# A slot of every second block moved from TensorE's pick to Pool's gather, in the two aggregation phases of a graph network

## The reference, cut to what matters

```python
def mean_aggregate(x, src, dst, num_nodes):
    msgs = x[src]
    summed = jax.ops.segment_sum(msgs, dst, num_segments=num_nodes)
    deg = jax.ops.segment_sum(jnp.ones((src.shape[0],), x.dtype), dst, num_segments=num_nodes)
    return summed / jnp.maximum(deg, 1.0)[:, None]
```

## Time and profile before

| | us |
|---|---|
| median of 3 timed runs | 9398.32 (9396.81 to 9399.93) |
| the profiled execution's own time | 9389.86 |
| its span, first to last instruction | 9388.1 |
| PE busy in the span | 8537.5 (91%) |
| PEld busy | 7847.4 (84%) |
| POOL busy | 6558.1 (70%) |
| DVE busy | 6333.0 (67%) |
| ACT busy | 5621.9 (60%) |
| mean granted TensorE clock, share of full | 0.951 |

### The profile page before, as it was taken

One profiled execution on the slowest core, in us unless ns is written; L12 is line 12 of the kernel. 1 busy time (PEld: TensorE's weight loads), 2 busy tenths in 40 slices (PEclk: granted clock), 3 DMA queues, 4 the chain that ended last, 5 costly groups with the idle time before them and its releaser, 6 DMA issues. The chain is left out here.

```text
span 9388.1 us, 166017 instructions
## 1 busy us (share of the span) xinstructions
PE 8537.5 (91%) x52125; PEld 7847.4 (84%) x52126; DVE 6333.0 (67%) x7523; ACT 5621.9 (60%) x10160; POOL 6558.1 (70%) x6704
## 2 busy tenths in 40 slices
PE   6999999998879999999898878888888888999997
PEld 6999999888879999999888857777777777888886
DVE  4666666766766666667767666666666666777776
ACT  3666666555537666665555436666666666666664
POOL 3777777765637777777666447777777777777774
PEclk9999999999979999999999979899999999999998
DMA  3222222111112222221111122222222222222221
GB/s 61 48 49 48 49 47 50 42 39 36 39 29 50 47 48 49 47 50 44 40 38 37 31 70 57 57 56 54 57 57 57 57 57 57 55 55 57 57 57 50
DMA packets 404389, 466.17 MB, mean 50 GB/s; under 512 B 194789, under 2 KB 273209, under 8 KB 403942
## 3 DMA queue, kind: packets, MB, share of 16 engines
q0 software_dynamic: 212000, 156.07, 10.8%
q1 hardware_dynamic: 190388, 308.83, 10.5%
q10 hardware_dynamic: 1938, 0.49, 0.0%
HBM read 451.33 MB, written 13.55 MB: 50 GB/s over the span
## 5 line engine op out<-in xcount | busy, mean ns | idle before, releaser
L636 PE MATMUL banks<-split_sb,e_low_hot 128*128 128x400 f32 x20000 | 4283.2, 358 | 40.0 <-ACT e_low_hot L606 40.0
L636 PEld LDWEIGHTS banks<-split_sb,e_low_hot 128*128 128x128 f32 x20000 | 3796.7, 192 | 83.6 <-ACT e_low_hot L606 40.5
L855 POOL DMA_INDIRECT big<-hn_table,src_i x2875 | 2853.5, 993 | 884.8 <-issue 869.6
L606 ACT ACTIVATE e_low_hot<-e_key_off 128x1536 fp32r<-128x1536 f16 x1000 | 1272.2, 1272 | 1851.9 <-PE banks L639 1820.7
L581 POOL DMA_INDIRECT big<-p_table,src_i x1875 | 1807.6, 964 | 756.3 <-issue 556.2
L581 POOL DMA_INDIRECT big<-h_table,src_i x1875 | 1806.5, 963 | 727.7 <-issue 559.0
L688 DVE TENSOR_REDUCE picked<-banks 128x48 f32<-128x1200 f32 x1000 | 1194.2, 1194 | 1204.0 <-PE banks L639 1201.0
L602 ACT ACTIVATE e_key_off<-e_key_in,node_off 128x384 f16<-128x384 f16 (+1 forms) x4000 | 1920.8, 550 | 114.6 <-DMA e_hi_in<-sel_dram 32.8
L708 DVE SCALAR_TENSOR_TENSOR hot<-dst_f,win_base,banks 128x1536 bf16<-128x1536 f32 (+1 forms) x934 | 1762.5, 1896 | 310.3 <-issue 181.2
L890 PE MATMUL banks<-hn_split,e_low_hot 128*128 128x448 f32 x7000 | 1487.4, 369 | 73.5 <-issue 68.3
L890 PEld LDWEIGHTS banks<-hn_split,e_low_hot 128*128 128x128 f32 x7000 | 1298.7, 188 | 202.2 <-issue 61.8
(11 more groups left out here) (208 smaller groups left out, 5989.4 us busy)
## 6 DMA issues: line engine op xcount, KB each, us to landing
e_wide<-in_edge_t SPq DMA_DIRECT2D x125, 832.0 KB
e_key_in<-sel_dram SPq DMA_DIRECT2D x250, 320.0 KB
e_hi_in<-sel_dram SPq DMA_DIRECT2D x250, 320.0 KB
big<-hn_table,src_i POOLq DMA_INDIRECT x2875
big<-p_table,src_i POOLq DMA_INDIRECT x1875
big<-h_table,src_i POOLq DMA_INDIRECT x1875
e_key_in<-gate_dram SPq DMA_DIRECT2D x125, 64.0 KB
src_i<-in_src SPq DMA_DIRECT2D x375, 12.5 KB, 1.7
```

What stands on the lines that cost most here:

```text
L606: act.activation(low_hot[gr][:, :, :], off, ACT.Relu, bias=1.0, scale=-1.0).then_inc(low_made, 1)
L636: pe.matmul(o, low_hot[gr][:, h, e], split_sb[:, h:HI1 * HI2:HI2, part * H:(part + 1) * H], start=(h == 0 and part == 0), stop=False)
L855: pool.indirect_dma_start(buf[u][:, j, 0:F], None, table, bass.IndirectOffsetOnAxis(ap=src_i[u][:, j:j + 1], axis=0),).then_inc(gathered[u ...
```

## The change

In blocks with an odd number (u is 1 or 3) the fourth group has one slot instead of two, so that TensorE picks nine slots; the last slot, j = 24, is gathered by POOL as the sixteenth. Even blocks stay as they were. The waits for the gathers count 16 in odd blocks; ACT, DVE and PE work on the smaller width in the fourth group of odd blocks, and `parts` on nine slots there. The core of the diff:

```diff
+LESS = 1
...
-            took = SLOTS - SEL
+            def size(gr, u):
+                return SIZE[gr] - (LESS if u % 2 == 1 and gr == NGR - 1 else 0)
+
+            def picks(u):
+                return sum(size(gr, u) for gr in range(NGR))
+
+            def took(u):
+                return SLOTS - picks(u)
...
-                            sp.wait_ge(gathered[u], 16 * took * (g + 1))
+                            sp.wait_ge(gathered[u], 16 * took(u) * (g + 1))
...
-                        for j in range(took):
+                        for j in tuple(range(SLOTS - SEL)) + tuple(range(SLOTS - SEL + picks(u), SLOTS)):
...
                     def low_hots(gr, n, turn, u):
-                        es = slice(AT[gr] * P, (AT[gr] + SIZE[gr]) * P)
-                        off = key_off[:, :, 0:SIZE[gr] * P]
+                        w = size(gr, u) * P
+                        es = slice(AT[gr] * P, AT[gr] * P + w)
+                        off = key_off[:, :, 0:w]
...
-                        act.activation(low_hot[gr][:, :, :], off, ACT.Relu, bias=1.0,
+                        act.activation(low_hot[gr][:, :, 0:w], off, ACT.Relu, bias=1.0,
...
-                        for k in range(SIZE[gr]):
+                        for k in range(size(gr, u)):
...
-                        pe.wait_ge(gathered[u], 16 * took * (g + 1))
+                        pe.wait_ge(gathered[u], 16 * took(u) * (g + 1))
...
                         if inside(n + 1):
-                            pick(0, n + 1)
+                            pick(0, n + 1, u + 1)
                         add_up(n, g, u)
                         if inside(n + 1):
-                            pick(1, n + 1)
-                            pick(2, n + 1)
-                            pick(3, n + 1)
+                            pick(1, n + 1, u + 1)
+                            pick(2, n + 1, u + 1)
+                            pick(3, n + 1, u + 1)
...
-                    def take(gr, n):
+                    def take(gr, n, u):
+                        k = size(gr, u)
                         dve.wait_ge(pick_psum, NGR * n + gr + 1)
-                        found = banks[:, BANK0[gr] * 512:(BANK0[gr] + SIZE[gr]) * 512].rearrange(
+                        found = banks[:, BANK0[gr] * 512:(BANK0[gr] + k) * 512].rearrange(
...
                     def parts(u):
-                        o = buf[u][:, SLOTS - SEL:, :]
+                        m = picks(u)
+                        o = buf[u][:, SLOTS - SEL:SLOTS - SEL + m, :]
                         dve.drain()
-                        dve.tensor_copy(o[:, :, HI:HI + H], picked[:, :, :])
+                        dve.tensor_copy(o[:, :, HI:HI + H], picked[:, 0:m, :])
```

More of the change, by code:

```diff
@@ L625, in _, with pick @@
                     pe.sem_inc(hot_used[1], 1)
-                    def pick(gr, n):
+                    def pick(gr, n, u):
                         pe.wait_ge(low_made, NGR * n + gr + 1)
@@ L659, in body @@
                         if inside(n + 1):
-                            pick(0, n + 1)
+                            pick(0, n + 1, u + 1)
                         add_up(n, g, u)
                         if inside(n + 1):
-                            pick(1, n + 1)
-                            pick(2, n + 1)
-                            pick(3, n + 1)
+                            pick(1, n + 1, u + 1)
+                            pick(2, n + 1, u + 1)
+                            pick(3, n + 1, u + 1)
                     for gr in range(NGR):
-                        pick(gr, 0)
+                        pick(gr, 0, 0)
                     with pe.Fori(0, turns) as g:
@@ L677, in high_hots @@
                     def high_hots(gr, turn, u):
-                        es = slice(AT[gr] * P, (AT[gr] + SIZE[gr]) * P)
+                        w = size(gr, u) * P
+                        es = slice(AT[gr] * P, AT[gr] * P + w)
                         if gr == 0:
                             dve.wait_ge(keys_in[u], 32 * turn)
-                        dve.tensor_scalar(hi_hot[gr][:, :], hi_in[u][:, es], hi_key[:, :], None,
+                        dve.tensor_scalar(hi_hot[gr][:, 0:w], hi_in[u][:, es], hi_key[:, :], None,
@@ L682, in high_hots @@
                                           ALU.is_equal).then_inc(hi_made, 1)
-                    def take(gr, n):
+                    def take(gr, n, u):
+                        k = size(gr, u)
                         dve.wait_ge(pick_psum, NGR * n + gr + 1)
-                        found = banks[:, BANK0[gr] * 512:(BANK0[gr] + SIZE[gr]) * 512].rearrange(
+                        found = banks[:, BANK0[gr] * 512:(BANK0[gr] + k) * 512].rearrange(
                             "p (s c) -> p s c", c=512)[:, :, 0:PICK].rearrange("p s (a f) -> p s f a", f=H)
-                        dve.tensor_reduce(picked[:, AT[gr]:AT[gr] + SIZE[gr], :], found, AX.X,
+                        dve.tensor_reduce(picked[:, AT[gr]:AT[gr] + k, :], found, AX.X,
@@ L689, in take @@
                                           ALU.max).then_inc(pick_taken, 1)
                     def parts(u):
-                        o = buf[u][:, SLOTS - SEL:, :]
+                        m = picks(u)
+                        o = buf[u][:, SLOTS - SEL:SLOTS - SEL + m, :]
                         dve.drain()
-                        dve.tensor_copy(o[:, :, HI:HI + H], picked[:, :, :])
+                        dve.tensor_copy(o[:, :, HI:HI + H], picked[:, 0:m, :])
                         dve.drain()
-                        dve.tensor_tensor(rest[:, :, :], picked[:, :, :], o[:, :, HI:HI + H], ALU.subtract)
+                        dve.tensor_tensor(rest[:, 0:m, :], picked[:, 0:m, :], o[:, :, HI:HI + H], ALU.subtract)
@@ L697, in parts @@
                         dve.drain()
-                        dve.tensor_copy(o[:, :, MID:MID + H], rest[:, :, :])
+                        dve.tensor_copy(o[:, :, MID:MID + H], rest[:, 0:m, :])
                         dve.drain()
-                        dve.tensor_tensor(o[:, :, LO:LO + H], rest[:, :, :], o[:, :, MID:MID + H],
+                        dve.tensor_tensor(o[:, :, LO:LO + H], rest[:, 0:m, :], o[:, :, MID:MID + H],
                                           ALU.subtract).then_inc(msgs_made, 1)
@@ L716, in body @@
                         make_hot(0, n, 0, since + 1)
-                        take(3, n)
+                        take(3, n, u)
                         if inside(n + 1):
@@ L737, in body @@
                             for gr in range(3):
-                                take(gr, n + 1)
+                                take(gr, n + 1, u + 1)
                                 if inside(n + 2):
@@ L744, in _ @@
                     for u in range(bufs):
-                        dve.memset(buf[u][:, SLOTS - SEL:, ONES:LO], 1.0)
+                        dve.memset(buf[u][:, SLOTS - SEL:SLOTS - SEL + picks(u), ONES:LO], 1.0)
                     dve.sem_inc(pick_taken, 2)
@@ L749, in _ @@
                     for gr in range(3):
-                        take(gr, 0)
+                        take(gr, 0, 0)
                         high_hots(gr, 1, 1)
```

## The result

The changed kernel takes 9465.9 us (median of four runs, 9458.1 to 9479.0) against 9397.6 for the kernel before: +68 us, ratio 1.0075 with a 95% interval of 1.0063 to 1.0087. It is slower, as forecast. The forecast was +52.8 us and 9450 us, the range 9418 to 9488.

A forecast was written before the change was run, and what follows sets the result against it. POOL was taken to bound blocks 56 to 78, the PE and DVE chain those behind. Two phases of 49.3 - 23.6 + 0.7 give +52.8 us on 9398.3, rounded to 9450 us, range 9418 to 9488.

The forecast's parts named there:

- What bounds the kernel: POOL bounds blocks 56 to 78 at 18.95 us a block; from 78 on the chain of PE and DVE does.
- The sixteenth gather: In odd blocks before 78 each extra gather is on the path: 39 x 1.263 = 49.3 us a phase slower.
- The late gain: Blocks 79 to 123: one slot of picks less gains 1.04 us per odd two-window block, 23.6 us a phase.
- the wait of 0.59 us: Odd late blocks: DVE's next half 0 is held by PE; an earlier `add_up` removes this, counted as 0.55 us.
- The tenth of `parts`: Odd late blocks: DVE's `parts` gets a tenth cheaper with one slot less, 0.08 us.
- the clock's: Early dips get absorbed by odd blocks' slack except at block 78, 0.7 us a phase; no added late dips counted.
- rival 2: Late blocks: the clock gets worse, odd blocks have twice the dips, +41 us in all, 9491 us; chance 0.09.
- The hand-over term: At block 78 a clock dip's delay may stay: 0 to 1.4 us a phase, taken as 0.7.
- the costs put at nothing: ACT's narrower one-hots, smaller memset, DVE's high one-hot, DMA load and stages outside e1 and e2: no effect.
- Rival 1: Late blocks: the whole slot of 1.69 us counts in 23 odd blocks a phase, +21 us, 9419 us; chance 0.09.
- Rival 3: Late blocks: the new rhythm avoids clock dips of 0.89 us a block, -84 us if all went, 9367 us; chance 0.03.
- Rival 4: Early blocks: the extra gather is hidden and PE's smaller work counts, -106 us, 9292 us; chance 0.02.

The follow-up runs named there:

- the added part alone: Kernel before plus a sixteenth gather into a spare tile in odd blocks, TensorE still picking ten slots: 9489.8 us, ratio 1.0104.
- the runs with filler: Eight constant matmuls ahead of second windows from block 80 on: kernel before 9313.5 us, changed kernel 9359.4, change in late blocks alone 9269.3; with four there, 9273.0.

## Why the prediction was right, and where a term was off

**What bounds the kernel.** Right in both stretches. POOL bounds the early one: PE's nine matmuls a slot are worth nothing there (the added part alone gives the same early stretch as the whole change), and late the extra gather costs nothing that shows (0 to 4.3 us a phase with the added part alone, in the first of which 10 us more were throttled than before).

**The sixteenth gather**, 49.3 us a phase: measured 46.0 and 48.8, and 47.4 and 47.1 with the change in early blocks alone. Three of the four lie below 48.8, which the prediction called the least. The price of 1.263 us was right; the rest of the gathers got a little cheaper, which the sum had at nothing: 1224 gathers in 1683.9 - 136.0 us are 1.265 each, 1185 in 1637.2 - 135.6 before were 1.267. The rule of the Trainium skill (SBUF — State Buffer, "Who interferes with whom") that a cast of VectorE locks the gathers out, worked out as 61 us in the prediction, doesn't show at that size: the median gather is 955 ns in both phases of both kernels, and the longest are 1321 and 1148 ns after, 1267 and 1318 before.

**The late gain.** The chain was right: the wait of 0.59 us went, the take got 0.41 cheaper, and with the clock at 1.00 the gain is 20 to 22 us for 23.6. The tenth of `parts` (0.08) wasn't there, see the last section. **The term that was off is the clock's.** The prediction put more dips in the late blocks at nothing and gave them, as rival 2, a chance of 0.09. In the profiled execution the throttled time there rose from 99.6 and 96.6 to 140.4 and 137.0 us, which took 17 us a phase of the 22, and e1's last block began at 2771 us instead of 2756. Rival 2 had the place right; its price (41 us in all) was near the 2 x 17 that the profile shows.

The Trainium skill (TensorE: Matmul & The Clock Gate, "Why this matters for your kernels") warns against idle gaps of PE between bursts. The gaps that it warns of are longer than the 1.76 us here, so the runs with filler agree with its direction and not with its size: clock 1.00 where it was 0.94.

**How much of the closeness is luck.** Over the runs the loss is smaller than in the two profiled executions, of which that of the kernel before is faster than all its timed runs and that of the changed one above its median. By the medians 68.4 us were measured, 15.6 more than forecast. The kernels with filler split that: without dips the change costs 45.9, which is 6.9 less than the forecast, and the dips add 22.5, some 11 a phase or half of the late gain. So a clock term that was missing is in part hidden by a sum that was otherwise too high, and the 15.6 flatters the forecast.

Why the dips spread when PE's idle time in an adding-up grew only by some 0.3 us is only partly known. With four short matmuls in front of the second window they are gone, so they go with the idle time there. Before, undisturbed blocks (22 of the 43 blocks 80 to 122 in e1) and blocks with a dip mixed; after, 38 of the same 43 had one, and blocks 95 to 120 come in a fixed pair of 24.8 and 23.0 us, where the kernel with filler has pairs of 23.4 and 21.6. In that part the clock records start a dip every 23.9 us, which is the mean of the pair; in the kernel before, the dips of the late stretch were mostly 23.9, 47.8 or 71.7 us apart. So loop and dips seem to run in step after the change, each dip keeping the block long enough to meet the next. That is a reading of the records; no run here tested it.

**The hand-over term** of 0.7 us and the costs put at nothing (ACT's one-hots, the stages outside e1 and e2) can't be told from nothing: outside the four stretches the two profiled spans differ by 2.3 us.

**The other rivals.** Rival 1 (the whole slot counts) is out: no more than 22 us a phase comes even at clock 1.00, and 1.69 x 23 would be 39. Rival 3 (the new rhythm avoids the dips) is out: it met more. Rival 4 is out by the early stretches.

## What to carry to other kernels

When work moves between two engines, count for each stretch which engine's part arrives first at the joint, not which is busier: POOL at 76% was the bound beside PE at 99.7%, and the move should be made only in those blocks in which the receiver has slack. Here that is the same edit behind block 80, and it is faster where the whole edit is slower. When a change makes PE wait more often for a microsecond or two, count the granted clock as a cost of its own; a few matmuls of constants inside the wait brought 80 us on the kernel before, and made the late part of the edit worth 44 us (9313.5 to 9269.3) instead of 24.

## What the runs showed of the hardware that wasn't expected

- A wait of 1.76 us once in a block of 23 us, with shorter ones beside it, goes with a mean granted clock of 0.94 to 0.96; four matmuls, 1.0 us, inside it bring the clock to 1.00.
- DVE's cast of 128x144 takes longer than that of 128x160, 303 ns against 271 and 277 in the mean over the changed kernel. That eats what the subtractions save: the four instructions of `parts` take 1.23 us in odd blocks and 1.21 in even ones, where the prediction took off 0.08. No run here shows the cause. The rows of the changed kernel (count, then busy us and mean ns):

```profile
L711 DVE CAST big<-rest 128x144 bf16<-128x144 f32 x124 | 37.6, 303 | 9.1
L707 DVE CAST big<-picked 128x144 bf16<-128x144 f32 x124 | 37.5, 303 | 11.3
L711 DVE CAST big<-rest 128x160 bf16<-128x160 f32 x126 | 34.9, 277 | 9.2
L707 DVE CAST big<-picked 128x160 bf16<-128x160 f32 x126 | 34.1, 271 | 11.5
```

- One chip ran the same program 42% slower, 13.3 ms, both times that it was used, with PE idle between matmuls with no wait that the profile shows. No run here shows the cause.
